# Second norm's rows and the router in three bf16 parts, turned by DMA; first norm's halves in one step (one core, gated cross-attention and mixture of experts)

## What is computed

```python
x = x + tanh(g_xattn) * attention(layernorm(x), ctx_512, ...)   # 16 heads of 128x128 scores, per batch
x = x + tanh(g_ffn) * ffn(layernorm(x), router, ...)            # x_flat: 4096 rows

# ffn
logits = x_flat @ router                       # [4096, 512] @ [512, 8]
topk_logits, sel = top_k(logits, 2)            # two of eight experts for each row
cw = softmax(topk_logits)
y = routed experts (capacity 1280 rows each) weighted by cw + shared expert
```

## Time and profile before

| | |
|---|---|
| median of 3 runs | 1970.11 us (1969.35 to 1971.21) |
| the profiled execution | 1971.24 us, of it 1969.4 us from first to last instruction |
| mean granted TensorE clock | 0.993 |
| PE, busy | 1896.2 us, 96% |
| PEld (weight loads) | 1061.5 us, 54% |
| DVE | 947.8 us, 48% |
| ACT | 665.0 us, 34% |
| POOL | 604.3 us, 31% |

### The profile page before, as it was taken

How to read it: one execution, slowest core, us unless ns; L and a number is a source line. 1 busy time by engine, 2 the same in 40 slices (tenths; PEclk the granted TensorE clock), 3 DMA queues, 4 the chain that set the end, 5 groups by cost and what they waited for, 6 DMA issues and landing times.

```text
span 1969.4 us, 32020 instructions
## 1 busy us (share of the span) xinstructions
PE 1896.2 (96%) x11801; PEld 1061.5 (54%) x11972; DVE 947.8 (48%) x1802; ACT 665.0 (34%) x1905; POOL 604.3 (31%) x651
## 2 busy tenths in 40 slices
PE   7799999999999999999999999999999999999999
PEld 7455566665666655444445555555544444444444
DVE  4776677676766666567332222222224424333333
ACT  4655655656566666420112222222210000000000
POOL 4544444444444455200223434433111111010101
PEclk9999999999999999999999999999999999999999
DMA  9454555554555565442359999899832532121202
GB/s 300 114 105 109 108 110 107 108 109 114 116 117 116 121 121 129 105 123 81 79 120 224 256 218 220 213 223 222 181 107 97 107 88 82 29 86 33 75 23 85
DMA packets 427299, 250.01 MB, mean 127 GB/s; under 512 B 360368, under 2 KB 366256, under 8 KB 427184
## 3 DMA queue, kind: packets, MB, share of 16 engines
q1 hardware_dynamic: 415664, 210.61, 46.3%
q0 software_dynamic: 11520, 37.76, 7.1%
HBM read 113.02 MB, written 48.23 MB: 82 GB/s over the span
## 4 chain that ended last, share of the span: by engine, by line
PE 59%; issue 13%; DVE 12%; POOL 7%; ACT 6%; DMA 1%; SPq 1%; DVEq 0%; POOLq 0%; ACTq 0%
PE score L725 11%; PE o L815 8%; PE score L804 7%; DVE arena L1015 6%; PE o L737 6%; PE p_bank L725 6%; PE m_bank L725 5%; ACT arena L892 4%; PE p_bank L804 4%; PE m_bank L804 4%; POOL arena L1383 3%; PE c_bank L737 3%; PE t_bank L737 3%; DVE arena L1095 2%; ACT arena L909 1%
## 5 line engine op out<-in xcount | busy, mean ns | idle before, releaser
L583 PE MATMUL o<-arena 128*128 128x512 bf16 x1473 | 341.1, 381 | 4.2 <-issue 0.4
L1015 DVE TENSOR_TENSOR arena<-arena 128x512 bf16<-128x512 f32 (+2 forms) x347 | 280.1, 813 | 72.1 <-ACT arena L845 55.2
L892 ACT ACTIVATE arena<-score,arena 128x128 f32<-128x128 f32 x512 | 181.6, 368 | 224.7 <-DVE arena L1095 224.6
L1383 POOL TENSOR_TENSOR arena<-arena 128x512 f32<-128x512 f32 x128 | 157.1, 1227 | 326.0 <-DVE arena L1036 324.1
L725 PE MATMUL score<-arena 128*128 128x512 bf16 x1037 | 234.3, 379 | 2.4 <-DMA arena<-xn_d 1.4
L583 PEld LDWEIGHTS o<-arena 128*128 128x128 bf16 x1536 | 151.0, 100 | 155.9 <-issue 2.8
L632 PE MATMUL p_bank<-arena 128*128 128x256 bf16 x1536 | 180.7, 275 | 0.7 <-DVE arena L1015 0.7
L725 PEld LDWEIGHTS score<-arena 128*128 128x128 bf16 x1056 | 103.3, 98 | 126.7 <-DMA arena<-xn_d 1.5
L815 PE MATMUL o<-arena 128*128 128x512 bf16 (+1 forms) x681 | 160.0, 379 | 2.0
L632 PEld LDWEIGHTS p_bank<-arena 128*128 128x128 bf16 x1536 | 146.2, 98 | 24.6 <-DVE arena L1015 1.0
L1469 POOL TENSOR_TENSOR arena<-arena 128x1088 bf16<-128x1088 f32 x32 | 72.0, 2250 | 274.5 <-ACT arena L922 274.5
(11 more groups left out here) (160 smaller groups left out, 2680.3 us busy)
## 6 DMA issues: line engine op xcount, KB each, us to landing
xrow_d<-arena SPq DMA_DIRECT2D x80, 256.0 KB, 3.6
arena<-w_expert SPq DMA_DIRECT2D x32, 544.0 KB, 5.2
arena<-w_shared SPq DMA_DIRECT2D x22, 384.0 KB, 3.4
arena<-x SPq DMA_DIRECT2D x16, 512.0 KB, 5.1
arena<-x SPq DMA_DIRECT2D x32, 256.0 KB, 5.2
x_d<-arena SPq DMA_DIRECT2D x32, 256.0 KB, 2.4
xn_d<-arena SPq DMA_DIRECT2D x32, 256.0 KB, 2.5
arena<-x_d SPq DMA_DIRECT2D x8, 1024.0 KB, 6.2
```

What stands on the lines that cost most here:

```text
L583: mm = pe.matmul(o_bank[b % 2][:, :], lhsT=cT[u % 2][:, a, h, :], rhs=M_w[:, w, head_of(hg, h), :], start=(hg == 0 and n == 0), stop=(hg = ...
L892: mm = act.activation(prob[:, u % 4, h, :], score_bank[u % 2][:, h * S:(h + 1) * S], ACT.Exp, bias=neg_max[:, u % 4, h:h + 1], accum_out=d ...
L1015: return dve.tensor_tensor(dst, src, hi, ALU.subtract)
L1383: pool.tensor_tensor(prob[:, u % 4], prob[:, u % 4], rden[:, u % 4, :].unsqueeze(2).broadcast_to([P, 4, S]), ALU.mult).then_inc(normed, 1)
```

## The change

- `xn2_rows` has three parts in place of two. ScalarE casts the upper part of the second norm in m=2 (batch of even number) and m=3 (odd); GpSimd subtracts it from `xn2` in place; ScalarE casts the middle part from that in m=3 and m=4; GpSimd subtracts again and writes the last part. `norm_2` moves from m=2 and m=3 to the ends of m=1 and m=2.
- SyncE, in m=4 and m=6, stores the first two parts and turns all three by one DMA transpose into `xT2` (12 blocks of 128x128, bf16), after a wait for the router product of the batch before.
- The router is split once into three bf16 parts that stand side by side (24 columns). TensorE multiplies the 12 turned blocks with it in m=5 and m=7, all in one PSUM group. VectorE sums the three groups of 8 columns into the logits in m=6 and m=0. The fp32 transposes, the fp32 router products and ScalarE's copies of both are gone.
- The first norm's upper halves move on ScalarE to just after the probabilities' cast of m=2, its lower halves on VectorE ahead of the piece's lower half of m=2.
- At the end VectorE leaves its steps 134 and 135 until after the first hidden layer of the shared experts, and sums the last logits there.
- Two fp32 uses of TensorE stay: the fusing of weights at the start (L690) and the ranks of the router (L764).

The diff, cut:

```diff
         xn2 = words(2 * D).rearrange("p (b n) -> p b n", b=2)
-        xT32 = words(2 * D).rearrange("p (b n) -> p b n", b=2)
-        xn2_rows = [halves(words(D)).rearrange("p (l n) -> p l n", l=2) for _ in range(2)]
+        xn2_rows = [halves(words(3 * D // 2)).rearrange("p (l n) -> p l n", l=3) for _ in range(2)]
+        xT2 = halves(words(768)).rearrange("p (l t n) -> p l t n", l=3, t=KT)
...
@@ SyncE, step
-                if m in (6, 7):
-                    b = 2 * (k // 8 - 1) + m - 6
+                if m in (4, 6):
+                    b = 2 * (k // 8 - 1) + (m - 4) // 2
                     if within(b, NB):
                         wait(sp, xn2_lo, b + 1, 4, it)
                         sp.dma_start(xn2_b[at(b, 4, it)],
-                                     xn2_rows[b % 2].rearrange("p l n -> p (l n)")).then_inc(xn2_out[b % 2], 16)
+                                     xn2_rows[b % 2][:, 0:2, :].rearrange("p l n -> p (l n)"))\
+                            .then_inc(xn2_out[b % 2], 16)
+                        wait(sp, lg_mm, b, 4, it)
+                        if it is not None:
+                            sp.sem_inc(turn_begun, 1)
+                        sp.dma_start_transpose(xT2.rearrange("p l t n -> p (l t) n"),
+                                               xn2_rows[b % 2].rearrange("p l n -> p (l n)")).then_inc(xT2_in, 16)
@@ TensorE, misc
-                if m in (4, 5):
-                    b = 2 * (c - 1) + m - 4
+                if m in (5, 7):
+                    b = 2 * (c - 1) + (m - 5) // 2
                     if within(b, NB):
-                        wait(pe, xn2_ready, b + 1, 4, it)
-                        misc_free(b, 2 * (c - 1), it)
-                        ln_transposes(xn2[:, b % 2, :], l2_mm)
-                if m in (6, 7):
...
-                            mm = pe.matmul(m_bank[:, 0:E], lhsT=xT32[:, b % 2, t * P:(t + 1) * P],
-                                           rhs=router_sb[:, t * E:(t + 1) * E], start=(t == 0), stop=(t == KT - 1))
+                        wait(pe, xT2_in, 16 * (b + 1), 64, it)
+                        wait(pe, lg_up, b, 4, it)
+                        if b == 0:
+                            pe.wait_ge(router_split, 5)
+                        for n in range(3 * KT):
+                            mm = pe.matmul(m_bank[:, 0:3 * E], lhsT=xT2[:, n // KT, n % KT, :],
+                                           rhs=router_w[:, n % KT].rearrange("p w e -> p (w e)"),
+                                           start=(n == 0), stop=(n == 3 * KT - 1))
                         mm.then_inc(lg_mm, 1)
@@ ScalarE, step, after the probabilities' upper half
+                if m == 2 and within(c + 2, NG):
+                    g = c + 2
+                    wait(act, xT1_in[(g - 1) % 2], 32 * ((g - 1) // 2 + 1), 32, it)
+                    for s in range(2):
+                        wait(act, xn1_ready, 2 * g + s + 1, 4, it)
+                        act.copy(xn1_rows[s][:, HI, :], x_ln[:, s, :]).then_inc(xn1_hi, 1)
@@ ScalarE, step, after the piece's upper half (the same five lines of xn1 removed there)
-                if m in (4, 5):
-                    b = 2 * (c - 1) + m - 4
+                if m in (3, 4):
+                    b = 2 * (c - 1) + m - 3
+                    if within(b, NB):
+                        wait(act, xn2_rest, b + 1, 4, it)
+                        act.copy(xn2_rows[b % 2][:, 1, :], xn2[:, b % 2, :]).then_inc(xn2_mid, 1)
+                if m in (2, 3):
+                    b = 2 * (c - 1) + m - 2
                     if within(b, NB):
                         wait(act, xn2_ready, b + 1, 4, it)
                         wait(act, xn2_out[b % 2], 16 * (b // 2), 32, it)
+                        wait(act, xT2_in, 16 * (b - 1), 64, it)
                         act.copy(xn2_rows[b % 2][:, HI, :], xn2[:, b % 2, :]).then_inc(xn2_hi, 1)
-                        wait(act, l2_mm, b + 1, 4, it)
-                        act.copy(xT32[:, b % 2, :], m_bank[:, :]).then_inc(l2_up, 1)
-                if m in (6, 7):
...
@@ VectorE, step
-                if m in (2, 3):
-                    norm_2(m - 2, g2, g1, it)
+                if m == 2 and within(c + 2, NG):
+                    for s in range(2):
+                        wait(dve, xn1_hi, 2 * (c + 2) + s + 1, 4, it)
+                        lower(xn1_rows[s][:, LO, :], x_ln[:, s, :], xn1_rows[s][:, HI, :]).then_inc(xn1_lo, 1)
                 q = k + 12
...
-                if m == 2 and within(c + 2, NG):
-                    for s in range(2):
...
                 if m == 1:
                     norm_1(g1, it)
+                    norm_2(0, g2, g1, it)
+                if m == 2:
+                    norm_2(1, g2, g1, it)
...
+                if m in (6, 0):
+                    b = 2 * (c - 1) if m == 6 else 2 * c - 3
+                    if within(b, NB):
+                        wait(dve, lg_mm, b + 1, 4, it)
+                        parts = m_bank[:, 0:3 * E].rearrange("p (w e) -> p e w", w=3)
+                        dve.tensor_reduce(logits[:, b, :] if it is None else logits[:, bass.ds(at(b, 4, it), 1), :],
+                                          parts if it is None else parts.unsqueeze(1), AX.X, ALU.add)\
+                            .then_inc(lg_up, 1)
@@ VectorE, before the loop
+            dve.wait_ge(const_in, 64)
+            for i in range(3):
+                ins = dve.tensor_copy(router_w[:, :, i, :], router_sb)
+                ins.then_inc(router_split, 1)
+                if i < 2:
+                    dve.wait_ge(router_split, 2 * i + 1)
+                    dve.tensor_tensor(router_sb, router_sb, router_w[:, :, i, :], ALU.subtract)\
+                        .then_inc(router_split, 1)
+                    dve.wait_ge(router_split, 2 * i + 2)
-            run_steps(dve, step)
+            run_steps(dve, step, LAST_STEP - 2)
@@ GpSimd, step, after the probabilities
-                if m in (4, 5):
-                    b = 2 * (c - 1) + m - 4
+                if m in (3, 4):
+                    b = 2 * (c - 1) + m - 3
+                    if within(b, NB):
+                        wait(pool, xn2_mid, b + 1, 4, it)
+                        pool.tensor_tensor(xn2_rows[b % 2][:, 2, :], xn2[:, b % 2, :], xn2_rows[b % 2][:, 1, :],
+                                           ALU.subtract).then_inc(xn2_lo, 1)
+                if m in (2, 3):
+                    b = 2 * (c - 1) + m - 2
                     if within(b, NB):
                         wait(pool, xn2_hi, b + 1, 4, it)
-                        pool.tensor_tensor(xn2_rows[b % 2][:, LO, :], xn2[:, b % 2, :], xn2_rows[b % 2][:, HI, :],
-                                           ALU.subtract).then_inc(xn2_lo, 1)
+                        pool.tensor_tensor(xn2[:, b % 2, :], xn2[:, b % 2, :], xn2_rows[b % 2][:, HI, :],
+                                           ALU.subtract).then_inc(xn2_rest, 1)
```

More of the change, by code:

```diff
@@ L80, in build @@
         table_sb = words(4 * P)
-        router_sb = words(KT * E)
+        router_sb = words(KT * E).rearrange("p (t e) -> p t e", t=KT)
+        router_w = halves(words(KT * 3 * E // 2)).rearrange("p (t w e) -> p t w e", t=KT, w=3)
         gate_sb = words(2)
@@ L255, in build @@
         pr_mm, pr_hi, pr_lo = sem("pr_mm"), sem("pr_hi"), sem("pr_lo")
[L256 removed]
+        xn2_rest, xn2_mid, xn2_lo = sem("xn2_rest"), sem("xn2_mid"), sem("xn2_lo")
+        xT2_in, router_split = sem("xT2_in"), sem("router_split")
         xn1_hi, xn1_lo = sem("xn1_hi"), sem("xn1_lo")
@@ L460, in _ @@
             sp.dma_start(gate_sb, gates).then_inc(const_in, 16)
-            sp.dma_start(router_sb.rearrange("p (t e) -> p t e", t=KT),
-                         router.rearrange("(t p) e -> p t e", t=KT)).then_inc(const_in, 16)
+            sp.dma_start(router_sb, router.rearrange("(t p) e -> p t e", t=KT)).then_inc(const_in, 16)
             for h in range(4):
@@ L642, in step @@
                 misc(k, it)
-            def misc_free(b, bl, it):
-                for s, c, top in ((l2_up, b, NB), (lg_up, bl, NB)):
-                    wait(pe, s, min(c, top) if it is None else c, 4, it)
             def misc(k, it):
@@ L651, in misc @@
                 c = k // 8
-                if m in (4, 5):
-                    b = 2 * (c - 1) + m - 4
+                if m in (5, 7):
+                    b = 2 * (c - 1) + (m - 5) // 2
                     if within(b, NB):
-                        wait(pe, xn2_ready, b + 1, 4, it)
-                        misc_free(b, 2 * (c - 1), it)
-                        ln_transposes(xn2[:, b % 2, :], l2_mm)
-                if m in (6, 7):
-                    b = 2 * (c - 1) + m - 6
-                    if within(b, NB):
-                        wait(pe, l2_up, b + 1, 4, it)
-                        misc_free(2 * c, b, it)
-                        for t in range(KT):
-                            mm = pe.matmul(m_bank[:, 0:E], lhsT=xT32[:, b % 2, t * P:(t + 1) * P],
```

(17 more changed lines are left out.)

13 lines of the change are left out of this document (1 added, 12 removed).

## The result

The changed kernel takes 1980.88 us (median of five runs, 1979.21 to 1984.41), the kernel before, on the same chip, 1969.35 us (five runs, 1968.27 to 1971.21): a ratio of 1.0061, 95% interval 1.0049 to 1.0073. It is slower by 0.6%, as forecast (1979 us, range 1963 to 1990). The profiled execution took 1980.11 us, with a span of 1978.3 us, against 1971.24 and 1969.4 before.

The account below looks back on a forecast made before the run. A circle of elementwise work on GpSimd, ScalarE and VectorE was taken to bound the kernel, with TensorE's savings counted as 0. Loop +7.8, fourteenth period +1.6, start -1 and end +0.7 sum to +9.1 on 1970.1: 1979 us, range 1963 to 1990.

Parts of the forecast that it names:

- What bounds the kernel: In the loop, a closed circle of elementwise work on GpSimd, ScalarE and VectorE sets the period; TensorE is just inside it.
- Part 1: TensorE's work: 0.8 us a batch saved, 26 us over 32, counted as 0 in the loop because it becomes waiting.
- Part 2: The loop's elementwise work on ScalarE, VectorE and GpSimd: the period grows by +0.6 us.
- (a): Up to ScalarE's piece split in m=2: the first norm's casts delay the contexts' split; about +0.8 us.
- (b): ScalarE's piece split, m=2 to m=3: GpSimd's subtraction holds norm_2; a gain of 0.74 us becomes a loss of 0.11.
- (c): ScalarE's piece split, m=3 to m=4: norm_2 leaves m=3, and the two splits come 0.27 us closer.
- (d): ScalarE's piece split, m=4 to the next m=2: middle part replaces upper part ahead of GpSimd's rope; no change.
- Part 3: SyncE's queue in m=4 and m=6: store and turn cost 0; up to 1 us a period if twice as slow.
- rival (3): SyncE's turn lands over 6 us after issue, holding probabilities or routers; 1 us more costs 1 us a period; 1985 to 1995; chance 0.10.
- Part 4: Whole run, start and end: 13 periods +7.8, fourteenth +1.6, start about -1, end +0.7; sum +9.1 us.
- (1): VectorE's norm_2 goes ahead of GpSimd's subtraction: period -0.24 us, 1967 us (1965 to 1971); chance 0.20.
- (2): TensorE is the bound after all: gain of 26 us, 1944 us (1925 to 1958); chance 0.12.

Follow-up runs that it names:

- e_one_product: Kernel before with only the first of a batch's four fp32 router products done (three quarters of each logit's sum left out): 1967.60 us, ratio 0.9983.
- e_vector_first: Changed kernel with norm_2 of the second batch moved ahead of the piece's lower half of m=2 on VectorE: 1968.73 us, ratio 0.9990.
- e_turn_first: Changed kernel with SyncE's three loads of m=4 issued behind that step's store and turn: 1980.03 us, ratio 1.0050.
- e_gpsimd_later: Changed kernel with GpSimd's subtraction of the first batch's upper part moved to m=3, behind the probabilities: 1974.67 us, ratio 1.0021.
- e_both: Changed kernel with norm_2 of the second batch ahead of the piece's lower half and SyncE's m=4 loads behind the turn: 1964.39 us, ratio 0.9980.
- e_before_plus: Kernel before with the first norm's halves moved and both norm_2 behind its lower halves in m=2, second norm still fp32 on TensorE: 1954.40 us, ratio 0.9926.
- e_second_norm_only: Changed kernel with the first norm's halves put back behind the piece's split of m=2: 2001.83 us, ratio 1.0161.

## Why the prediction was right

**What bounds the kernel.** Right. Taking products from TensorE left the period where it was (e_one_product), moving two lines of VectorE changed it by 1.2 us (e_vector_first), and the fastest kernel of all has the busiest TensorE in the loop. The 96% was no evidence of a bound. One sign of the prediction, TensorE busy under 94%, is there in the loop (454.7 of 495 us, 92%, from 205 to 700), not over the whole span (95%).

**Part 1.** Right. The 12 products take 0.31 us from the router's start to the next group's, 26 ns each, where 0.43 us was taken, the upper bound. It changes nothing in the sum, since TensorE's time counted as 0. The Trainium skill's floor of about 25 ns ("TensorE: Matmul & The Clock Gate", section "Wait — 56ns, not 53.3ns?") gave an estimated 0.30 us, and the trace agrees with it.

**Part 2 (a), (b), (c), (d).** Right, by the table of distances above: +0.81, +0.10, -0.24 and -0.06 where +0.8, +0.11, -0.27 and 0 were written. `norm_2` of the second batch took 1.39 us ("1.3 us or more"). The 0.05 us between GpSimd and VectorE came out as 299.96 and 300.01. That this order is the cause, and not only beside it, is shown by the two experiments that turn it round. The rule of the Trainium skill ("SBUF — State Buffer", section "SBUF: two separate sides") is that a VectorE instruction in a two-port mode or with two SBUF inputs and a GpSimd instruction exclude each other for a whole instruction, and the first to start has it. The 1.39 us and the two times 0.54 us agree with it; whether `norm_2` runs in a two-port mode no trace shows by itself. TensorE's stalls were to be 1.6, 0.9 and 1.4 us, ahead of m=1's piece, m=3's piece and m=4's scores. The second and third came out as 0.74 to 0.98 and 1.33 us. The first was 0.25 to 0.98 us in seven of the twelve periods and absent in five, in each of which the router had waited 1.42 us or more for the turn.

**Part 3.** The term that was wrong. It was counted at 0, with "under 1 us to spare" and "up to 1 us a period" if the turn were slow. The turn landed after 3.7, 5.1 and 7.5 us (least, median, most), where the kind in rows 9 has a median of 3.3, and of the 13 turns of step m=4 with c=1 to 13, the ones with loads ahead, seven passed the 6 us of rival (3). What it cost is far less than that rival's price of 1 us a period: 3.7 us in 12 periods. The text also said that such a wait "would lie in TensorE's idle time". Most of them do. What was left out is that a wait of 2.11 us is longer than that idle time (+0.8 us in its period), and that behind one of 1.88 us the clock fell, and the products behind it then didn't fit (+2.3). And the cause named was only the size of the turn; e_turn_first shows that the loads ahead of it in the queue are part of it.

**Part 4.** The loop's +7.8 is right (7.2 in the 12 periods that can be compared). The start was mis-sized: -1 was written, and the stall of m=4, c=1, comes at 161.38 after and 165.86 before, -4.5. With the first norm's part alone it is at 162.20, with the second norm's alone at 165.39, so it belongs to the first norm's part. The starts of ScalarE's piece splits show where most of it lies: the two steps from m=1 to m=3 with c=-1, where the pipeline fills, take 19.9 us before (58.19 to 78.08) and 16.7 after (57.37 to 74.05), and 17.0 with the first norm's part alone (58.41 to 75.39). Why they give 3 us there, and not the 0.5 of a later period, stays open. The end is near: from that stall in c=13 to the second group of the shared experts' products +2.7 (727.16 to 837.11 before, 733.55 to 846.22 after), against +1.6 for the fourteenth period, +0.6 for the thirteenth and +0.7 (whose own terms, 2 to 3 us less 1.3, give 0.7 to 1.7). TensorE waited 4.03 us for the transposed rows, after:

```profile
831.69 7.04 PE L719 MATMUL score<-arena 128*128 128x512 bf16 x24 [4.03 <-DMA arena<-xn_d]
```

against 1.44, and the 24 products took 7.04 us in place of 5.35 at the lower clock. In the profiled pair the difference of the times is 8.9 us, against 9.1 forecast: 7.2 + 3.7 - 4.5 + 2.7 - 0.2 behind the end. Between the medians it is 11.5 us, 2.4 over the forecast. Two errors, the turn's +3.7 and the start's -3.5, cancel; the nearness of the total is partly luck.

**Rivals.** (1) was excluded by the duration of `norm_2`, and its period, 46.4, is what e_gpsimd_later shows once the order is turned (46.43). (2) was excluded by e_one_product. (3) met its condition in about half of the turns of m=4, at a small part of its price. What is still open: where e_turn_first gives back most of the 1.8 us behind the loop, and what sets the end, which holds half of e_both's 10 us over e_before_plus. In the traces 4.3 of them are there by m=4 of c=13 (715.49 against 711.21; 0.39 us of period is most of it), and 5.0 more lie between there and the second group of the shared experts' products (112.97 against 107.95 us), where the turns and the loads share SyncE's queue. No run took the turns out of that queue.

## What to carry to other kernels

Before an engine is relieved, look for what its idle time waits for: here a TensorE that was busy for 96% had one short wait in each period, and the circle behind that wait, of ScalarE, VectorE and GpSimd, set the time. When elementwise work is moved between engines, write down the start of each instruction at its new place to 0.05 us and look at what the other of VectorE and GpSimd starts at that moment; an instruction of 0.5 us that arrives just behind one of 1.2 us costs 1.4, and the same instruction one place earlier costs nothing. A change of two parts should be timed by its parts: one of these two was worth -9 us and the other +31.

## What the runs showed of the hardware that was not expected

- A short wait of TensorE can cost twice, and its length alone does not tell. After waits of 1.88 us (after, at 265) and 2.52 us (e_second_norm_only, at 265) the granted clock of the 3 us from 265 and from 267 was 0.71 and 0.65, and what had taken 2.75 and 2.79 us took 4.44 and 4.01. But after waits of 2.11 and 1.86 us (after, at 362 and 647) it stayed at 1.00, and the stall of 2.52 us in each of twelve periods was followed by a fall in five. Before, with its wait of 1.6 us in every period, the granted clock is 1.00 in each stretch of 50 us from 160 to 660.
- A DMA transpose from SBUF to SBUF of 12 blocks of 128x128 bf16 landed 3.7 to 7.5 us after its issue, median 5.1, where in the loop every second one had three loads ahead of it in the same queue; with the loads behind it, 3.7 to 5.9, median 4.3.
- 12 products of 24 columns in bf16 took 26 ns each from start to start, 0.31 us together, against 0.81 us for four fp32 products of 8 columns.
